# Both ends of an expert stage: a constant slot for the first tile, the last down weights split a step early, and second values made at the start of the last stage

## What is computed

```
x = x + tanh(g_xattn[0]) * attention0(layernorm(x), ctx)      # per token, over its 16 x 16 head grid
x = x + tanh(g_ffn[0])   * (shared(layernorm(x)) + expert[argmax](layernorm(x)))
x = x + tanh(g_xattn[1]) * attention1(ctx, ctx, layernorm(x)) # 512 x 512 per batch entry
x = x + tanh(g_ffn[1])   * butterfly_ffn(layernorm(x))
```

## Time and profile before

| | |
|---|---|
| median of 3 runs | 781.7 us (780.89 to 782.49) |
| profiled execution | 779.64 us, span 777.8 us |
| TensorE busy | 707.4 us, 91% |
| VectorE busy | 616.1 us, 79% |
| ScalarE busy | 368.7 us, 47% |
| GpSimd busy | 416.4 us, 54% |
| chain that ended last | TensorE 42%, VectorE 12%, issue 5%, ScalarE 5%, DMA 1% of the span |

### The profile page before, as it was taken

One profiled execution on the slowest core, in us unless ns is written; L12 is line 12 of the kernel. 1 busy time (PEld: TensorE's weight loads), 2 busy tenths in 40 slices (PEclk: granted clock), 3 DMA queues, 4 the chain that ended last, 5 costly groups with the idle time before them and its releaser, 6 DMA issues.

```text
span 777.8 us, 12689 instructions
## 1 busy us (share of the span) xinstructions
PE 707.4 (91%) x4359; PEld 589.0 (76%) x4359; DVE 616.1 (79%) x956; ACT 368.7 (47%) x635; POOL 416.4 (54%) x304
## 2 busy tenths in 40 slices
PE   4759999999999899799999999999876999999996
PEld 2438888788878789567777777777665989989996
DVE  4788999999999945889978888887667767687653
ACT  1313333333333321276666667777443666455643
POOL 4788898888889880406976666664022101110000
PEclk9769999999999999999999999999989999999999
DMA  9300000001036012133254415010010101000000
GB/s 298 146 21 22 21 22 21 20 23 38 20 102 271 8 61 68 41 163 115 104 190 190 190 42 224 28 28 15 14 34 28 35 21 56 28 28 8 15 15 20
DMA packets 24289, 54.32 MB, mean 70 GB/s; under 512 B 3152, under 2 KB 20304, under 8 KB 23088
## 3 DMA queue, kind: packets, MB, share of 16 engines
q1 hardware_dynamic: 19056, 45.54, 16.2%
q0 software_dynamic: 1872, 5.11, 2.3%
q10 hardware_dynamic: 3312, 3.02, 1.1%
HBM read 46.45 MB, written 7.21 MB: 69 GB/s over the span
## 4 chain that ended last, share of the span: by engine, by line
PE 42%; DVE 12%; issue 5%; ACT 5%; DMA 1%; POOL 0%; ACTq 0%; DVEq 0%; POOLq 0%
PE bank L716 16%; PE bank L707 13%; PE bank L947 8%; PE bank L724 3%; DVE SLOT_r L1826 2%; DVE PRODV_r L1826 2%; DVE STC L1900 1%; ACT L1365 1%; ACT XS L1365 1%; DVE NM L1950 1%; ACT SLOT_r L1369 1%; DVE X L1971 1%; DVE X L1922 1%; DVE SLOT L1968 1%; DVE MVC L1902 1%
## 5 line engine op out<-in xcount | busy, mean ns | idle before, releaser
L595 POOL TENSOR_TENSOR PRODV<-SHARED 128x2048 f32<-128x2048 f32 x32 | 144.5, 4516 | 28.4 <-DVE bank L1537 27.9
L707 PEld LDWEIGHTS bank<-ROWS,SLOT 128*128 128x128 f32 x1024 | 120.5, 194 | 1.6
L707 PE MATMUL bank<-ROWS,SLOT 128*128 128x128 f32 x1024 | 120.7, 277 | 0.0
L686 POOL TENSOR_TENSOR RS<-VE,MHALF 128x2 f32<-128x2 f32 x16 | 13.1, 821 | 153.5 <-DVE VE L1907 153.5
L707 PE MATMUL bank<-SLOT,XST 128*128 x184 | 84.6, 603 | 2.6 <-issue 2.6
L1459 DVE TENSOR_TENSOR PRODQ<-bank,SHARED 128x4096 f32<-128x4096 f32 x16 | 70.7, 4417 | 11.5 <-PE bank L707 11.5
L597 POOL TENSOR_TENSOR PRODV<-PRODV 128x1024 f32<-128x1024 f32 x32 | 74.8, 2337 | 2.5
L1468 DVE TENSOR_REDUCE bank<-PRODQ 128x256 f32<-128x4096 f32 x16 | 70.7, 4419 | 0.1
L1826 DVE TENSOR_TENSOR PRODQ_r<-SLOT,ROWS_r 128x1024 fp32r<-128x1024 f32 x46 | 66.1, 1438 | 0.6 <-ACT ROWS_r L1289 0.6
L610 POOL DMA_INDIRECT XS<-normal_rows,INV x23 | 27.2, 1184 | 72.3 <-PE bank L724 51.2
L1826 DVE TENSOR_TENSOR SHARED_r<-bank,HA_r 128x512 fp32r<-128x512 f32 x46 | 31.6, 686 | 40.1 <-ACT HA_r L1273 39.4
(11 more groups left out here) (249 smaller groups left out, 1848.0 us busy)
## 6 DMA issues: line engine op xcount, KB each, us to landing
SLOT<-wexp SPq DMA_DIRECT2D x9, 3072.0 KB, 11.4
X<-x SPq DMA_DIRECT2D x16, 128.0 KB, 2.2
SHARED<-ctxT SPq DMA_DIRECT2D x16, 128.0 KB, 2.4
normal_rows<-ROWS SPq DMA_DIRECT2D x16, 128.0 KB, 1.7
WET<-ctxT SPq DMA_DIRECT2D x4, 512.0 KB, 8.4
out<-X SPq DMA_DIRECT2D x16, 128.0 KB, 1.7
expert_rows<-YS ACTq DMA_DIRECT2D x12, 128.0 KB, 1.7
expert_rows<-PICK ACTq DMA_DIRECT2D x11, 128.0 KB, 2.7
```

The costliest lines, as they stand in the source:

```text
L595: gp.tensor_tensor(o, pr, v, ALU.mult).then_inc(s["av_prod"], 1)
L707: last = pe.matmul(dst, lhs(k), rhs(k), start=(k == 0), stop=(k == chunks - 1))
```

## The change

Start: TensorE does eight identity products (`warm`), then turns tile 0 and makes its queries before its keys and values; ScalarE turns tile 0 before it copies keys and values, and does the tanh after that.

Expert stage, front: tile 0 has slot 0 as a constant on TensorE, ScalarE and VectorE; TensorE waits for `tables` and loads the table after tile 0's h1 product. Low up weights of tile 0 go to FIRST2L (in W0), so VectorE waits for `e_down` only at tile 1. `first_stage` for tile 0 moves to the end of its step.

Expert stage, end: the down weights of the last tile are split one step early, into LAST3H (in ROWS) and LAST3L (in PRODV). In the last step four of the eight fold turns are done ahead of the down product on TensorE, with their copies on ScalarE.

Last stage: V1 and V1L have two buffers; contexts of entries 0 and 1 are both split before the stage, and the values of entry 1 are made there too, no longer in unit 1. Fold banks are PB 1 to 4, the ring is PB 6, 7, 4. SP's and GpSimd's code is the same.

The core of the diff:

```diff
+        FIRST2L = W0[:, :].rearrange("p (k f) -> p k f", k=KD)
+        LAST3H = ROWS[:, 0:KF * D].rearrange("p (k d) -> p k d", k=KF)
+        LAST3L = flatV[:, KF * D:2 * KF * D].rearrange("p (k d) -> p k d", k=KF)
...
-        CTXH = [EB[:, 0, :].rearrange("p (k t) -> p k t", k=KD), CTXL1]
+        V1L = [SHARED[:, r * TB * D:(r + 1) * TB * D].rearrange("p (t d) -> p t d", t=TB) for r in range(2)]
+        CTXH = [W0[:, 0:KD * L].rearrange("p (k t) -> p k t", k=KD), CTXL1]
...
-                if u % 2 and u + 1 < UNITS:
+                if u > 1 and u % 2 and u + 1 < UNITS:
                     uses += [("values", (u + 1) // 2, r) for r in range(2)]
...
-        RING = [PB[n] for n in (4, 6, 7)]
+        RING = [PB[n] for n in (6, 7, 4)]
...
-        FOLD = [PB[n] for n in (6, 7, 1, 2)]
+        FOLD = [PB[n] for n in (1, 2, 3, 4)]
...
@@ TensorE, attention step
+                if t0 is not None and first(t0, 1):
+                    warm(PB[0], 8)
+                    turned(t0)
+                    pe.wait_ge(w_in, 32)
+                    queries(t0)
...
+            def warm(bank, n):
+
+                for _ in range(n):
+                    pe.matmul(bank[:, 0:P], IDENT[:, :], IDENT[:, :], start=True, stop=True)
...
@@ TensorE, expert stage
-                slot = held_for.pop(n)[0]
+                slot = held_for.pop(n)[0] if n else 0
...
                 if t0 is not None:
+                    if n == 0:
+                        pe.wait_ge(tables, 1)
                     held_for[n + 1] = placed(n + 1)
                     expert_flip(t0)
...
-                    pe.wait_ge(tables, 1)
-                    held_for[0] = placed(0)
                 if t2 is not None:
+                    if n2 == NT - 1:
+                        for n in range(4):
+                            fold_turn(n)
                     expert_down(t2)
...
@@ TensorE, before the last stage
-            fold_down()
+            for n in range(4, KF):
+                fold_turn(n)
             pe.wait_ge(pair_split, 2)
             values(0, 0)
+            pe.wait_ge(e["by_sb"], NT)
+            values(0, 1)
             pe.wait_ge(wm_sb, KF)
-            values(0, 1)
             fold(0)
+            for r in range(2):
+                values(1, r)
...
@@ ScalarE, expert step
-                if t2 is not None:
+                if t2 is not None and num(t2) < NT - 1:
                     down_weights(t2, 0)
                     turned_hidden(t2, 0)
                     turned_hidden(t2, 1)
                     down_weights(t2, 1)
+                elif t2 is not None:
+                    turned_hidden(t2, 0)
+                    turned_hidden(t2, 1)
+                    for n in range(4):
+                        turned_fold(n)
...
+                if t1 is not None and num(t1) == NT - 1:
+                    down_weights(t1, 0)
+                    down_weights(t1, 1)
                 if t2 is not None:
                     expert_rows(t2)
...
@@ VectorE, expert step
-                    if first(t0, 1):
-                        dve.wait_ge(late_in, 16 * 4)
-                        dve.wait_ge(z_in, 16)
-                        first_stage(0)
...
+                if t1 is not None and num(t1) == NT - 1:
+                    lower_down(t1, 0)
+                    lower_down(t1, 1)
+                if t0 is not None and first(t0, 4):
+                    if first(t0, 1):
+                        dve.wait_ge(late_in, 16 * 4)
+                        dve.wait_ge(z_in, 16)
                     first_stage(num(t0))
...
@@ VectorE, before the last stage
+            for n in range(4):
+                lower_turned_fold(n)
+            dve.wait_ge(slot_uses, NT)
+            split_context(0)
...
+            for n in range(4, KF):
+                lower_turned_fold(n)
+            dve.wait_ge(slot_uses, NT + 1)
+            split_context(1)
...
             lower_values(0, 0)
+            lower_values(0, 1)
+            lower_fold(0)
             next_rows(0)
             next_stats(0)
-            lower_values(0, 1)
+            lower_values(1, 0)
             norm_rows(0, 0, "c_rstd", "c_xT", "c_xn")
-            lower_fold(0)
+            lower_values(1, 1)
```

154 lines of the change are left out of this document (88 added, 66 removed).

## The result

| | before | changed |
|---|---|---|
| median of the runs | 781.49 us (780.89 to 782.49, 4 runs) | 773.86 us (773.18 to 774.37, 4 runs) |
| ratio to before | | 0.990 (0.9888 to 0.9913) |
| profiled execution | 779.64 us, span 777.8 | 773.89 us, span 772.1 |

The change is faster by 7.6 us, 1.0%. The forecast was 771.6 with a range of 767.5 to 776: the side was right and the time lies in the range, 2.3 us above the forecast. The sum itself was made against the profiled execution and said 10.1; between the two profiled executions only 5.7 us went. That the median fell by 7.6 is because the profiled execution of before lies 1.9 us under its median and that of the change does not. So part of the closeness of the forecast is luck: term by term it is 4.4 us off.

A forecast was written before the change was run, and what follows sets the result against it. Bounds: VectorE, with GpSimd close behind, in attention; TensorE in the expert stage except its ends and later in the last stage. -0.9 - 1.6 - 4.3 - 3.3 = -10.1, giving 771.6 us for the median, range 767.5 to 776.

The forecast's parts named there:

- Start, -0.9: Start and attention: first scores 2.2 us earlier by queries first, 0.9 of it left; range +0.5 to -2.2.
- a first query product of 2.07: Start, named sign of being wrong: TensorE's clock still low, first scores at 13.3, a loss of 0.5 us.
- the fast case: Start: after the identity products, queries take 1.13 and keys and values 1.88 us; first scores at 10.7 instead of 12.85.
- Front, -1.6: Expert stage, front: second tile's product at 332.5 instead of 334.06, with VectorE the bound; range -0.8 to -3.6 us.
- The collision: Expert stage, front: VectorE's low parts of the up weights meet GpSimd's product and end at 327.0, undelayed at 324.6.
- End, -4.3: Expert stage, end: down product ends 4.8 us earlier, VectorE 0.5 late in the pause; range -2.0 to -5.5 us.
- Last stage, -3.3: Last stage: 0.95 us from the context split leaving the first unit, 2.36 from values leaving the second; -2.4 to -3.8.
- The pause does not absorb: Rival, pause before the last stage: context splits, second values or low clock cost time there; 775.7 us, chance 0.15.
- Nothing at the ends: Rival, expert stage's ends: the 2.13 us reappears, the down product waits for something else; 777 us, chance 0.03.
- GpSimd's folded matrix: Slower rival, last down product: fold transposes before it wait for this matrix if over 24 us later; 786.7, chance 0.03.

The follow-up runs named there:

- f_loads_old: Changed kernel, but TensorE again waits for the tables and loads tile 0's slot from the table before the first product; 776.31 us, ratio 0.9937.
- g_wait: Changed kernel, but GpSimd's last growth product waits until VectorE's low parts of the first up weights are done; 772.83 us, ratio 0.9896.
- s_old: Changed kernel with the start as before: keys and values first, no identity products, tanh first; 774.96 us, ratio 0.9929.
- s_nowarm: Changed kernel without the eight identity products at the start; 774.11 us, ratio 0.9907.
- a_again: The changed kernel once more, nothing altered; 773.28 us, ratio 0.9905.
- e_old: Changed kernel, but the last tile's down weights are split in the last expert step again, fold blocks left moved; 775.44 us, ratio 0.9929.
- v_old: Changed kernel, but the second values (entry 1) are made in the last stage's unit 1 again; 778.58 us, ratio 0.9957.
- f_stage_late: Changed kernel with VectorE's first stage for tile 0 one step later, directly before that for tile 1; 771.91 us, ratio 0.9884.

## Why the prediction was right or wrong

**Start, -0.9, measured +0.7 in the profiled execution.** The step that failed is "the pair products still wait for their last input until 16.50. The first exponential stands behind their copies on ScalarE at 22.88". I left their duration at what it was with 1.97 us of idle time before them, and had moved 2.7 us of work away from just there. With 4.70 us idle the clock was low for most of 14 to 22 (0.58), and they ended at 23.94 instead of 22.69. The idle time alone does not settle how much falls into the low clock: with 4.54 us in f_loads_old the two groups of eight take 3.47 and 1.89 us, where they take 3.78 and 2.74 here. Where less of them fell into the low clock (g_wait: 16.15 to 22.23) the last row update came at 317.58, and over nine traces with the new start it lies between 317.58 and 320.12, at 318.9 in the mean; two of before gave 319.01 and 319.63, s_old 320.23. So the term is about -0.5 in the mean, its sign was right, and the single trace on which I would have judged it is at the bad end. That last row update follows GpSimd's first product by 294.7 to 295.5 us in all fourteen traces: that product's start is the number to forecast. The identity products, which I counted at nothing lost, bring little or nothing either (s_nowarm). And the sign of being wrong that I named, a first query product of 2.07, did come: 2.05 in a_again, and 2.04 to 2.05 in three more of the ten traces with them. That the fast case would be taken each time was a guess that the first trace happened to bear out.

**Front, -1.6, measured +0.7.** The collision was forecast and came so: low parts to end at 327.0, 8.0 us behind the cut; they ended at 327.4, 7.7 behind it. The Trainium skill (SBUF — State Buffer, "Who interferes with whom") says that a VectorE instruction with two SBUF inputs and a reading GpSimd instruction exclude each other; 4.49 and 2.99 us side by side, 2.64 and 2.19 apart, agree. What failed is "From there VectorE has the six moved instructions (2.0 to 2.5 ...), a low part of rows 0.4": from 327.3 to 330.33 it is 3.0, because the stage ends in a wait for its own last addition and a read of the next slot (0.96 together), which a sum of busy times does not hold. Part of the miss is arithmetic: the terms written down, from 327.0 on, add to 332.7 to 333.2 and not to 332.5. The second tile came at 334.05, late by 0.9 against the cut. The larger part is the clock: I let the low clock at the first product go (1.7 came) and did not ask where it would fall next. It fell on the second tile's product in the trace of the change (1.0 us, and 2.5 in a_again). This is no accident of one trace: in all eight with the change in which that product starts 14.2 to 14.4 us behind the cut it takes 4.51 to 6.15, in the four in which it starts at 11.2 to 13.9 it takes 3.60. In front of it TensorE idles 2.33 and then 1.08 in the changed kernel, 1.45 in the kernel before. So the late VectorE and the low clock came together, and the front of the changed kernel shows no clear gain: 233.98 and 235.56 us in its two traces, 233.32 and 234.24 in the two of before.

**End, -4.3, measured -3.7.** The down product was forecast at 558.5, 6.2 us behind the last tile's gate product, and came 6.2 behind it; 2.85 us long was forecast and 3.10 measured, the idle time of "about half a microsecond" was 0.50. Its end is 4.6 us earlier by the cut, 4.8 were forecast. VectorE was forecast 0.5 late in the pause and was not; instead the gather's transfer took 0.5 us longer. e_old shows the two halves of the 4.6: 2.5 us the early split (2.2 of them at the start), 2.1 the clock, kept there by the fold's blocks. The low clock behind the pause stayed in this trace, as forecast, but not in a_again, where its absence is worth 1.0.

**Last stage, -3.3, measured -3.4.** First unit 0.92 (0.95 forecast), second 2.46 (2.36). v_old confirms the second and that the first is not its doing. This term and the end's are right by mechanism and by size.

**The rivals.** "The pause does not absorb" fell: the first maximum stands as far behind the cut with the second values in the pause as without. "Nothing at the ends" is half true, by accounts that cancel: TensorE's 2.13 us went and reappeared as VectorE's time. GpSimd's folded matrix was never waited for. What no case of mine had is how far one execution of a kernel stands from the next: the front is 233.98 us in one trace of the changed kernel and 235.56 in the other.

## What to carry to other kernels

Taking time out before one wait makes the idle time before the next one longer; ask for each such stretch whether TensorE will come out of it at the low clock. Here the low clock took back 1 to 3 us at three places (the pair products, the second expert tile, the second tile of the first unit in f_stage_late). At the first two the record shows the longer idle time beside it (4.70 against 1.97 us, and 2.33 and 1.08 against 1.45); at the third TensorE's idle times before it (1.47 and 2.14) are those of the changed kernel, where the clock did not fall, so idle time is not the whole of it. Work moved on an engine that feeds another costs its own waits as well as its busy time, and a pair of engines that exclude each other pays the same price in any order, so the only way out is to put the collision where neither is waited for. Where a kernel's executions differ by 3 to 5 us, one trace of each does not settle a term of 1 us: count the same marker over all variants that share the stretch.

## What the runs showed of the hardware

VectorE's multiplications by a column (one SBUF tensor in, one out, 256 wide) also wait for GpSimd: 3.03 us for four in g_wait beside a product of 2.19, 1.14 for the next tile's four 9 us later with GpSimd idle. The Trainium skill (SBUF — State Buffer, "Who interferes with whom") lists this operation among those that can take the shared ports; the row agrees.

The exclusion can be followed instruction by instruction in the changed kernel. GpSimd's product starts at 323.30 and takes 2.99, 0.8 more than the 2.19 it takes in g_wait: that is the rest of VectorE's first low part (1.2 us from 322.88). The second low part then stands still until the product ends at 326.29 and ends 1.1 us behind it, at 327.37.

Small work can keep the clock: in e_old four blocks of transposes (1.04 us) and then 2.71 us of idle time left the down product at full clock, where 3.58 us of idle time without them had it at the low one (0.57 over 560 to 568, in the kernel before). That gave 2.1 us at the product's end. Eight identity products before the first tile did the same in six of ten traces (keys and values in 1.88 us against 3.54) and not in four (2.76 to 2.93); it gave the path nothing that the traces can tell from their spread, because there the path waited for something else. At the start only the durations tell the pace: the granted clock stands at 1.00 from 6 to 16 us in the kernel before, while the same product takes 3.65 and then 1.88.
